# Adapter attention: unturned scores over 16 rows per head in place of 32, and no reset of the seventeenth column

## The reference, cut to what matters

```
q, k, v = multilora(norm(x), ...)        # x W^T + (x A^T) B^T, adapter by batch
q, k    = rope(q), rope(k)               # per head, over the 16 values
scores  = q @ k^T * 16 ** -0.5           # 512 x 512 per head, causal
out     = softmax(scores) @ v
x       = x + multilora(out, ...)
```

## Time and profile before

| | |
|---|---|
| median of 3 runs | 2471.41 us (2469.82 to 2472.45) |
| profiled execution, its own time | 2469.7 us |
| its span, first to last instruction | 2468.0 us |
| mean granted TensorE clock | 0.905 |
| TensorE products busy | 2014.9 us (82%), 10760 instructions |
| TensorE weight loads busy | 1270.0 us (51%) |
| VectorE busy | 1087.4 us (44%) |
| ScalarE busy | 794.2 us (32%) |
| GpSimd busy | 527.0 us (21%), 612 instructions |
| unturned scores, line 2375 | 512 products, 103.7 us busy |
| turned scores, line 2380 | 512 products, 102.5 us busy |

### The profile page before, as it was taken

One profiled execution on the slowest core, in us unless ns is written; L12 is line 12 of the kernel. 1 busy time (PEld: TensorE's weight loads), 2 busy tenths in 40 slices (PEclk: granted clock), 3 DMA queues, 4 the chain that ended last, 5 costly groups with the idle time before them and its releaser, 6 DMA issues. The chain is left out here.

```text
span 2468.0 us, 30465 instructions
## 1 busy us (share of the span) xinstructions
PE 2014.9 (82%) x10760; PEld 1270.0 (51%) x10760; DVE 1087.4 (44%) x2229; ACT 794.2 (32%) x1743; POOL 527.0 (21%) x612
## 2 busy tenths in 40 slices
PE   7999999995699999989989965777656388889553
PEld 4565565654367757757857752232233144445332
DVE  4545545454521331241241144488644644445354
ACT  3535444441233243143233212411113234335232
POOL 2323323221200110020020000144311433342212
PEclk9999999998799999989989988999866689999666
DMA  5000000002000000000000000000000000000001
GB/s 235 1 1 1 1 1 1 1 1 90 0 0 0 1 0 0 0 0 0 0 0 0 0 0 1 0 0 0 0 1 1 0 1 1 1 1 1 1 1 34
DMA packets 9680, 23.36 MB, mean 9 GB/s; under 512 B 2400, under 2 KB 6256, under 8 KB 8816
## 3 DMA queue, kind: packets, MB, share of 16 engines
q1 hardware_dynamic: 8288, 18.92, 2.1%
q10 hardware_dynamic: 1296, 3.18, 0.4%
HBM read 20.00 MB, written 2.10 MB: 9 GB/s over the span
## 5 line engine op out<-in xcount | busy, mean ns | idle before, releaser
L967 ACT ACTIVATE cos_probs<-cos_ps 128x512 f32<-128x512 f32 x256 | 152.9, 597 | 280.2 <-PE cos_ps L1044 280.2
L1052 PEld LDWEIGHTS cos_ps<-cos_vx,cos_probs 128*128 128x128 f32 x2048 | 233.7, 191 | 15.3 <-issue 15.3
L1044 PE MATMUL cos_ps<-cos_qT,cos_kT 128*128 x512 | 233.8, 611 | 3.7 <-ACT cos_qT L953 3.7
L1052 PE MATMUL cos_ps<-cos_vx,cos_probs 128*128 128x129 f32 x2048 | 233.9, 274 | 0.0
L366 ACT ACTIVATE probs<-sc,nmax 128x512 f32<-128x512 f32 (+3 forms) x256 | 132.6, 525 | 188.6 <-DVE nmax L229 186.6
L868 DVE RECIPROCAL cos_rl<-cos_ps 128x4 f32<-128x4 f32 x64 | 11.7, 183 | 383.4 <-PE cos_ps L1052 383.4
L473 PE MATMUL sc<-kT,qT 128*128 128x512 f32 (+3 forms) x512 | 172.4, 459 | 3.9 <-DVE probsT L241 2.5
L1044 PEld LDWEIGHTS cos_ps<-cos_qT,cos_kT 128*128 128x128 f32 x512 | 97.9, 196 | 117.5 <-issue 113.9
L2144 DVE TENSOR_REDUCE cos_wq<-lora_ps 128x2 f32<-128x1024 f32 (+3 forms) x128 | 101.9, 824 | 106.7 <-PE lora_ps L2387 105.7
L446 PE MATMUL pq<-xnT,wap 128*128 128x512 f32 x256 | 129.6, 631 | 3.7 <-DVE swp L221 3.3
L229 DVE TENSOR_REDUCE nmax<-sc 128x1 f32<-128x512 f32 (+3 forms) x256 | 112.5, 484 | 34.0 <-PE sc L475 31.3
(11 more groups left out here) (495 smaller groups left out, 3472.0 us busy)
## 6 DMA issues: line engine op xcount, KB each, us to landing
onT<-in_mla_wqT SPq DMA_DIRECT2D x1, 2048.0 KB, 9.8
mla_wo<-in_mla_wo SPq DMA_DIRECT2D x1, 2048.0 KB, 20.0
cos_wq<-in_cos_wq SPq DMA_DIRECT2D x1, 2048.0 KB, 25.7
cos_wout<-in_cos_wout SPq DMA_DIRECT2D x1, 2048.0 KB, 30.0
out<-x SPq DMA_DIRECT2D x1, 2048.0 KB, 7.5
x<-in_x SPq DMA_DIRECT2D x1, 1536.0 KB, 15.3
wq_pe<-in_mla_wq_pe ACTq DMA_DIRECT2D x1, 1024.0 KB, 14.8
x<-in_x SPq DMA_DIRECT2D x1, 512.0 KB, 4.6
```

The source lines that it names most:

```text
L967: act.activation(probs[:, j, kj, :], ps[:, kj, :], ACT.Exp).then_inc(s["e_ready"], 1)
L1044: pe.matmul(ps[:, kj, :], kT[:, kj * P:(kj + 1) * P], qT[:, 2 * p + j, :], start=True, stop=True).then_inc(s["s_ready"], 1)
L1052: last = pe.matmul(po[:, j, qi // 2, qi % 2, :], probs[:, j, kj, qi * P:(qi + 1) * P], vx[:, kj, :], start=(kj == 0), stop=(kj == TI - 1))
```

## The change

Two edits. In `turn_pairs`, the fill of the seventeenth column of `qs` with 0 for batches 2 and 3 is taken out. In `products`, the unturned scores read `LORA_HD` = 16 rows of each head's slot in `qT` and `kT`, from the slot's first row on, in place of `LORA_SLOT` = 32. The rows left out are the seventeenth (0 or a stale maximum in the queries, 1 in the keys) and the fifteen zero rows. The turned scores, the transposes, the mask product and every wait stay.

```diff
@@ -2193,8 +2193,6 @@
                 def turn_pairs(b, i):
                     pool.wait_ge(s["emptied_a"], emptied["qk", b, i])
-                    if b >= 2:
-                        pool.memset(qs[:, b % 2, i, :, LORA_HD:LORA_HD + 1], 0.0)
                     rotate(pool, raw[:, i, :], rot, i, slots(b, i), s["rope_done"])
@@ -2372,8 +2370,8 @@
                         if n <= LAST:
                             for j in range(2):
                                 r = LORA_SLOT * (mine_ + j)
-                                pe.matmul(ps[:, at + j, col:col + w], qT[r:r + LORA_SLOT, qi * P:(qi + 1) * P],
-                                          kT[r:r + LORA_SLOT, n % 2, 0:w], start=True, stop=False)
+                                pe.matmul(ps[:, at + j, col:col + w], qT[r:r + LORA_HD, qi * P:(qi + 1) * P],
+                                          kT[r:r + LORA_HD, n % 2, 0:w], start=True, stop=False)
```

## The result

The change made the kernel slower: 2477.23 us median of 9 runs (2476.03 to 2481.52) against 2472.13 us of the kernel before in the same rounds (2469.82 to 2474.89). The ratio is 1.0024, with a 95% interval of 1.0014 to 1.0034. The profiled execution took 2477.4 us, 7.7 more than that of before. Of this, 1.0 us lies ahead of the opening's scores (the first unturned products, which run alone); from the first of them to the end of the kernel it is 487.7 us against 481.1.

What follows compares the result with a forecast made beforehand. TensorE was taken to bound adapter attention, GpSimd in six iterations. Reset 0.5 us gained, sixteen rows 0, clock 0: 2471.4 - 0.5 = 2470.9 us (chance 0.52), range 2468.0 to 2478.0.

Steps and rivals of the forecast that it cites:

- What bounds the kernel: Adapter attention, about 1957 to 2310 us: TensorE bounds, busy 297.39 of 353 us, except in six iterations where GpSimd sets the end.
- the six waits: TensorE waiting for GpSimd's last causal selects before the product of probabilities and values, in six iterations: 24.4 us in all.
- The reset: Eight GpSimd fills in iterations 4, 5, 8 and 9: removing them gains 0.12 us a pair, 0.5 us in all.
- The product's duration: 512 unturned-score products on TensorE: 16 rows take as long as 32, columns set the time, so 0 us gain or loss.
- The rival in which they no longer overlap: Sixteen- and 32-row products no longer run side by side in 15 iterations: 97 us lost, 2568 us; chance 0.03.
- The clock: TensorE's granted clock in the opening and shared products: taken as unchanged by 16 rows, 0 us, since the row group is the same.
- shared products too: Rival: with 96 rows the clock also falls in products shared by unturned and turned scores; 6.2 us lost, 2477.6 us; chance 0.09.
- The opening was to cost 2.2 us: Rival: clock falls earlier in the first scores, which run alone; halfway costs 2.2 us, 2473.1, up to 2475.4; alone, chance 0.28.
- Three short falls at 1.5 us: First products behind a wait, in the slower rival: three low-clock places at 1.5 us each, added to the opening's 2.2 us.
- The price of attend: Product of probabilities and values (line 2335): 3.85 us at clock 0.50 against 2.36 at 1.00, so 1.5 us per low stretch.
- One sign of being wrong: Adapter attention: the prediction called itself wrong if the granted clock there is below 0.91.

## Why the prediction was wrong

**What bounds the kernel** was right, and borne out: the six waits were worth 31 us when they were taken away.

**The reset** was right by itself: 0.09 us a pair in the trace, for 0.12 in the sum. That it also moves where the clock falls, once the products have 16 rows, had no place in the sum; leaving it out saved 3.6 us of what 16 rows cost.

**The product's duration** was right: 0.70 and 0.59 us at full clock for either number of rows, and still side by side. The rival in which they no longer overlap is out.

**The clock** is the step that failed: its term was put at 0, and the runs show 5.7 us lost in iteration 6 and 1.2 by iteration 10, where shared products over 96 rows, or attend behind them, ran at half clock. "For the forecast I take 0: the sixteen-row instruction addresses the same row group, and every other duration that I can read is the same for both." Equal durations say nothing of what the clock follows, and the trace of before held the warning: a fall with TensorE busy for 9.80 of 10.00 us, among scores with only half the rows in use. I read it as a fall by rows, priced the two outcomes, and gave the right one 0.37 (0.28 and 0.09) where the wrong one got 0.52. The slower rival, "shared products too", forecast 2477.6 us with a chance of 0.09; the runs gave 2477.2. That its total came so near is luck, by errors that cancel. The opening was to cost 2.2 us and cost nothing (481.1 us from its first product to the end with either number of rows), since the stretch at half clock that began sooner also ended sooner. Three short falls at 1.5 us were assumed; there was one of 13.7 us, worth 5.7, and one lengthened from 3.4 to 6.8 us, worth 1.2. The fall in iteration 6 lasted through 9.7 us of products at 96 rows and ended 3.9 us into the transposes and projections over 128 rows behind them (they start at 2144.60, the clock is back at 2148.5). The price of attend, a product that uses all rows, was the wrong price for it. One sign of being wrong that the prediction named did show: the granted clock over adapter attention was 0.89 over 1957 to 2318 us, below 0.91.

The Trainium skill's "TensorE: Matmul & The Clock Gate", section "HAM oscillation — how this bites in real kernels", ties the loss of the clock to idle gaps. Behind the waits for GpSimd this trace agrees (3.44 us idle, then attend at 0.50). For the products it doesn't: the clock fell, and stayed at 0.50 for 13.40 us, with TensorE busy for 13.40 us. Here the measurement decides.

## What to carry to other kernels

Naming 16 rows in place of 32 in a product saved no time on TensorE here, and took away the clock for what stood near it; zero rows that are already there can be worth reading. When the granted clock falls while the engine is busy, look at how many rows the products in that stretch use, and measure it with more of them in use, if need be with work that nobody reads. Compare stretches that stand at the same distance behind the last return of the clock, and read more than one execution: two openings with the same rows, 0.8 us apart in that distance, went different ways here. Price such a fall by the products in which it would fall, not by others, and look for the work that would end it.

## What the runs showed of the hardware

The granted clock followed the rows that the products named, not the groups of 32 that they occupied: in the same groups, shared products with 128 and 112 rows in use kept 1.00 in iteration 6, with 96 they lost it for over 13 us, and with 66 they lost it for about 10 us in each of iterations 1, 2 and 3. Rows of zeros counted as rows. The falls recurred at the same places within 0.1 us, measured from the opening's first product, in separate executions of one kernel (two profiles each of the change and of its 16 rows alone), so that 0.5 us of work on another engine decided 3.6 us. It isn't so in every execution: the opening with 64 rows in use lost the clock 7.1 us into its scores in the kernel before and kept it in the profile of the run without the reset. How the rows and the place against the last return of the clock work together is open.
